# Six gathering stages of a graph network: each gather also waits for the gather two places ahead of it

## The reference

```python
h = relu(layernorm(x)); x = x + attention(h)       # layer 0: softmax over all edges, sums by src
h = relu(layernorm(x)); x = x + edge_mlp(h)        # layer 1: relu(concat(h[src], edge_attr) @ W1a + b1a) @ W1b, means by dst
h = relu(layernorm(x)); x = x + gatv2_twice(h)     # layer 2: logits of h[src] + h[dst] + e, softmax by dst, weighted sums
def edge_conv(x, W1, b1, W2, b2):                  # layer 3: three of these
    m = concat([x[dst], x[src] - x[dst]], axis=-1)
    return segment_max(relu(m @ W1 + b1) @ W2 + b2, dst)
```

## Time and profile before

| | us |
|---|---|
| median of 3 runs | 11882.29 (11880.79 to 11889.4) |
| span of the profiled execution | 11983.4 |
| busy in it: PE | 7468.0 (62%) |
| DVE | 6860.6 (57%) |
| POOL | 6587.1 (55%) |
| ACT | 2573.8 (21%) |

### The profile page before, as it was taken

One profiled execution on the slowest core, in us unless ns is written; L12 is line 12 of the kernel. 1 busy time (PEld: TensorE's weight loads), 2 busy tenths in 40 slices (PEclk: granted clock), 3 DMA queues, 4 the chain that ended last, 5 costly groups with the idle time before them and its releaser, 6 DMA issues. The chain is left out here.

```text
span 11983.4 us, 181872 instructions
## 1 busy us (share of the span) xinstructions
PE 7468.0 (62%) x39289; PEld 6257.1 (52%) x39290; DVE 6860.6 (57%) x13795; ACT 2573.8 (21%) x9089; POOL 6587.1 (55%) x6703
## 2 busy tenths in 40 slices
PE   5944444366665777736565554667777676766676
PEld 4944444355555555524454444655555555555555
DVE  6845444433335888866644445665555555565555
ACT  3500000111111000036600001333333233323332
POOL 0088888466651666613256663326666566646665
PEclk8956666555557888879976666779999899989998
DMA  4355555322223666645444443423333333333333
GB/s 124 73 96 96 96 95 95 98 66 66 67 58 76 216 215 213 219 85 160 128 119 127 127 128 100 113 79 130 129 131 130 118 131 129 129 117 130 131 131 120
DMA packets 829515, 1435.73 MB, mean 120 GB/s; under 512 B 184832, under 2 KB 495468, under 8 KB 788960
## 3 DMA queue, kind: packets, MB, share of 16 engines
q1 hardware_dynamic: 532336, 981.36, 25.8%
q0 software_dynamic: 297072, 453.23, 17.4%
HBM read 1114.85 MB, written 320.07 MB: 120 GB/s over the span
## 5 line engine op out<-in xcount | busy, mean ns | idle before, releaser
L1674 POOL DMA_INDIRECT T<-gather_d,srci x2508 | 2386.0, 951 | 1655.8 <-remote 618.6
L1723 PE MATMUL PS<-T,W 128*128 128x512 f32 x1248 | 816.5, 741 | 1102.5 <-issue 601.4
L882 POOL DMA_INDIRECT added_d<-T,slots x832 | 1293.7, 1555 | 284.0 <-issue 215.6
L1249 PE MATMUL PS<-T,ident 128*128 128x256 f32 (+1 forms) x3328 | 1086.0, 410 | 544.6 <-issue 377.1
L964 DVE TENSOR_TENSOR T<-T,PS 128x128 f32 (+1 forms) x2098 | 561.0, 286 | 1267.7 <-remote 935.2
L1247 PE MATMUL PS<-T 128*128 x3328 | 1050.4, 400 | 347.5 <-issue 343.7
L1198 POOL DMA_INDIRECT T<-wide_d,srci x832 | 844.2, 1015 | 686.0 <-PEq L71 267.6
L987 POOL DMA_INDIRECT T<-gather_d,srci x832 | 822.2, 988 | 583.9 <-issue 232.9
L1249 PEld LDWEIGHTS PS<-T,ident 128*128 128x128 f32 x3328 | 717.7, 244 | 768.7 <-issue 463.9
L1198 POOL DMA_INDIRECT T<-gather_d,srci x832 | 800.4, 962 | 578.8 <-issue 234.5
L1469 PE MATMUL PS<-T 128*128 128x260 f32 (+1 forms) x3328 | 758.5, 384 | 445.8 <-DVEq L1522 392.7
(11 more groups left out here) (254 smaller groups left out, 15227.1 us busy)
## 6 DMA issues: line engine op xcount, KB each, us to landing
T<-quads_d SPq DMA_DIRECT2D x315, 1024.0 KB
T<-edge_rows_d SPq DMA_DIRECT2D x210, 512.0 KB
edge_rows_d<-T SPq DMA_DIRECT2D x209, 512.0 KB
T<-onehot_t_d SPq DMA_DIRECT2D x416, 256.0 KB
T<-gather_d,srci POOLq DMA_INDIRECT x4172
T<-edge_rows_d SPq DMA_DIRECT2D x210, 256.0 KB
onehot_t_d<-T SPq DMA_DIRECT2D x208, 256.0 KB
edge_rows_d<-T SPq DMA_DIRECT2D x208, 256.0 KB
```

Source lines behind the costliest of these rows:

```text
L882: gp.indirect_dma_start(added_d[u][:, :], bass.IndirectOffsetOnAxis(ap=slots[:, k:k + 1], axis=0), part(OUT[r], u), None, compute_op=ALU.a ...
L1249: last = T_.matmul(spot(r, u), ident[:, :], part(R[r], u, width), start=False, stop=True)
L1674: gp.indirect_dma_start(part(R[n % RING], u), None, gather_d[:, :], bass.IndirectOffsetOnAxis(ap=srci[:, k:k + 1], axis=0)).then_inc(rows_ ...
L1723: T_.matmul(bank(2 + i), w2, RT[i], start=True, stop=True).then_inc(products_made.h, 1)
```

## The change

Before each gather of the six stages POOL also waits for the landing of the gather two places ahead of it in the order of the stage. The helper takes group n and place u and finds that gather's semaphore and count. Since a gather can so have two waits, the group's wait for its ring buffer gets an increment of `pool_gate` behind it, to stand on.

```diff
+        def landed_before(gp, n, u):
+
+            m, v = (n, u - 2) if u >= 2 else (n - 1, u + 2)
+            if m >= 0:
+                gp.wait_ge(rows_in[m % RING][v].h, rows_in[m % RING][v].at(16 * (m // RING) + 16))
+
         def edge_mlp_sums():
...
                     for n in range(GROUPS):
                         gp.wait_ge(rows_added.h, rows_added.done(n - RING))
+                        gp.sem_inc(pool_gate.h, 1)
                         for u in range(GROUP):
                             k = LEAD + n * GROUP + u
+                            landed_before(gp, n, u)
                             gp.indirect_dma_start(part(R[n % RING], u), None, gather_d[:, :],
...
+            pool_gate.passed(GROUPS)
...
                         gp.wait_ge(rows_free_again.h, rows_free_again.done(n - RING))
+                        gp.sem_inc(pool_gate.h, 1)
                         for u in range(GROUP):
                             k = step_of(n) + u
+                            landed_before(gp, n, u)
                             gp.indirect_dma_start(part(R[n % RING], u, width), None, table[:, :],
...
-            pool_gate.passed(GROUPS)
+            pool_gate.passed(2 * GROUPS)
...
                     for n in range(GROUPS + 1):
                         gp.wait_ge(edges_made.h, edges_made.done(n - RING))
+                        gp.sem_inc(pool_gate.h, 1)
                         for u in range(GROUP):
                             k = LEAD + n * GROUP + u
+                            landed_before(gp, n, u)
                             gp.indirect_dma_start(part(R[n % RING], u), None, gather_d[:, :],
...
+            pool_gate.passed(GROUPS + 1)
```

## The result

| | before | changed |
|---|---|---|
| median of 4 runs, us | 11881.54 (11862.51 to 11889.4) | 12834.28 (12826.13 to 12848.17) |
| span of the profiled execution, us | 11983.4 | 12835.6 |

The ratio is 1.0803, with a 95% interval of 1.079 to 1.0816. The sign was forecast; the time lies 709 us above the predicted 12125 and 74 us above the range.

What follows compares the result with a forecast made beforehand. Taken as bound by POOL's back-to-back gathers holding up the other engines until the ring fills. Terms -106, +144, -24 and +229 sum to +243 us, span 11983.4 to 12226, forecast 12125 us, range 11700 to 12760 us.

Steps and rivals of the forecast that it cites:

- The sign: Whole kernel: the change makes it slower, chance 0.74, against 0.18 for faster and 0.08 for within 0.2%.
- The wait binds, at 2.75 us for two gathers: POOL, unloaded gathering stage: waiting for landings makes two gathers take 2.75 us instead of 2.49.
- The rival in which it never binds: Six gathering stages: POOL sees landings within 2.49 us of the start, so all stays at 11882 us; chance 0.04.
- The increments cost nothing: POOL's queue, one pool_gate increment per group: taken as 0, with 375 us if every group stopped there.
- Most of the held-up time goes: Gathering stages: the slower gather stream mostly lets the other engines through; edge MLP stage at 1.41 us a gather, -106 us.
- Wide logits, 3.4 us a pair: Wide logits stage, 128 KB gathers beside stores and loads: 3.4 us for two, 1406 against 1262 us, +144.
- Narrow logits, 3.0 us a pair: Narrow logits stage: two gathers take 3.0 us, 1248 against 1272 us, -24.
- Maxima, 12.85 us for eight gathers: Three maxima stages: eight gathers at 1.375 us plus 1.85 us for meeting the 1 MB load; +76 each, +229 together.
- the rival in which gathers pass beside it: Maxima stages: gathers are little delayed by the 1 MB load and keep their pace; sum +14, 11896 us, chance 0.10.
- The carried 0.85%: Whole kernel: the profiled span's 0.85% excess over the median was carried over, turning 12226 us into 12125.
- others held up: Six stages: other engines stay held up, POOL's runs only get longer; sum +869 us, 12750 us, chance 0.24.

Runs made afterwards that it cites:

- e7: Changed kernel with each gather waiting for the landing of the one right ahead, so one gather at a time; 19631.12 us.
- e10: Changed kernel, unedited, run again beside new runs of the kernel before; 12741.65 us, ratio 1.1786 to the kernel before.
- e1: Changed kernel without its landing waits, keeping one pool_gate increment per group; 10825.91 us, ratio 1.0005 to the kernel before.
- e6: Changed kernel with a pool_gate increment ahead of each gather in place of the landing wait; 10826.8 us, ratio 1.0008 to the kernel before.
- e14: Changed kernel with 1 MB and one-hot loads cut to 8 of 128 partitions and each gather's rows stored separately; 11845.19 us (1 run).
- e3: Changed kernel with the 1 MB maxima loads and the one-hot logits loads cut to 8 of 128 partitions; 12067.47 us (1 run).
- e9: Kernel before the change, unedited, profiled again beside the experiments; 10803.36 us (1 run).
- e2: Changed kernel with the landing wait looking three places back, not two; 11428.38 us, ratio 1.0561 to the kernel before.

## Why the sign was right and the size wrong

The step that failed is the price of a landing wait where other transfers run: 3.4 us for two gathers in the wide logits stage, where 3.94 were measured, and 12.85 us for eight gathers in the maxima stages, where 13.7 were measured. The mechanism was right: POOL waits for landings, and that sets the pace.

- *The wait binds, at 2.75 us for two gathers.* Right: 2.77 in the timeline; 2.79 from start to awaiting start in e7; 2.82 over the edge MLP stage of e10. The rival in which it never binds fell.
- *The increments cost nothing.* Right, as far as these runs can tell (e1, e6).
- *Most of the held-up time goes.* As forecast for the maxima stages, only in part for the edge MLP stage: its pace was forecast at 1.41 us a gather, and e10 has 1175 / 832 = 1.41; but 74 us of pauses stayed in the first comparison. -30 in place of -106 us. In the maxima stages, too, some of these waits stayed ("remote" above), without a price that can be seen. This credit exists only against the first comparison's kernel before; beside e10, where the kernel before has no pauses, the same change costs 1930 us and not 953. Since that kernel can run without them, it is not shown that it was the change that took the pauses away.
- *Wide logits, 3.4 us a pair: the worst mis-sized term of a single stage.* 3.94 us were measured (1637 / 416), +382 in place of +144 us. Of the two latencies in the earlier trace rows I took the 3.12 and set the 4.93 aside as a crowd behind a pause that would not last. The 3.12 is close to the median landing in e10, but a group has two late gathers, at 4.33 and 3.89 us, and the wait passes them on. The crowd lasts: the landing that releases POOL also releases SP's store, once a group. With the store split and the load light it would have been 3.33 (e14), about what I took. The landings of L1209 in the wide stage of e10:

```profile
DMA to landing us min/median/max: 2.6/3.2/4.8
```

- *Narrow logits, 3.0 us a pair.* 3.12 (1297 / 416); +29 in place of -24 us, the same mistake in small (the second and third gather of a group landed in 3.16 and 2.99 us in e10, the others in 2.51).
- *Maxima, 12.85 us for eight gathers.* 13.7 us (1432 / 104.5). The meeting with the 1 MB load, taken as 1.85 us, measured 1.93 (e3), and the rival in which gathers pass beside it fell. The Trainium skill (DMA: Bandwidth & Descriptors, on queues, rings and completion order) says that an engine takes turns between queues packet by packet; what I had drawn from it, that a gather is delayed little, did not come true, for a gather that met the load was 2.6 us late. How the engines took turns no trace here shows. The rest was mis-sized: without most of the load eight gathers take 1230 / 104.5 = 11.8 us and not 11.0. 0.16 of it is the step of 2.79. For the rest, the trace of e3 has the awaited landing for 677 gathers of the first maxima stage: 520 of these waited for it, and the other 157 only for the end of the gather before; all but seven start within 0.31 us of whichever came last. So these steps too are landings, of which some come late (2.5 us in the median, a tenth above 2.9, 4.3 at most), and POOL's own pace behind them. How the 0.6 us divide between the two was not taken apart. In all +516 in place of +229 us. The landings of L1688 in that stage:

```profile
DMA to landing us min/median/max: 2.4/2.5/4.3
```

- *The carried 0.85%.* The changed kernel's profiled execution has next to none of it (12835.6 against a median of 12834.28), which is 100 us of the miss. The profiled execution of before was itself a longer one: its rest of the program took 4389.4 us, where e9 took 4346.5 and the changed kernel 4344.6.

By own spans the forecast was +243 and +852 came: 76 (edge MLP), 238 (wide), 53 (narrow) and 287 us (the three maxima stages together) too little, less 45 us that the rest of the program lost. With the 100 us this is the miss of 709. The rival with the nearest number, others held up (12750 us), is not what happened: outside the edge MLP stage, where 74 us of pauses stayed, POOL waits for landings, and the others follow at once.

## What to carry to other kernels

A wait for a transfer's landing costs the latency at its own place in the loop and not the median one (in the wide stage 3.2 us in the median, 4.33 for the second gather of a group), and a transfer that the same landing releases will be beside it each time: look for the queue that wakes on the same event. With a ring of four groups as the only bound, the 1 MB loads cost 14 to 24 us a stage; with two gathers in flight, 201 us. And before a loss in the kernel before is counted as something to win back, see whether it is there in another measurement, on another chip.

## What the runs showed of the hardware that was not expected

- The same kernel took 11881.54 us in one comparison and 10811.54 to 10825.76 us in four others on three chips. Of the 1182 us between the two profiled spans 1139 lie in the six gathering stages; in the timelines it is seen as a lag of 2.95 us (against 0.12) before other engines act on PE's signal, and in the waits as "remote", which stands in both traces of the first comparison and in none of the experiments. Even the changed kernel, which came out alike, has it in the first and not in e10. Neither the rate of gathers nor the loads bring it about by themselves, since e9 has both. What does is open.
- In the wide stage splitting the store saved 42 us and lightening the load 38 us, and the two together saved 253 us.
- TensorE's granted clock in the narrow stage is 0.64 on average in the kernel before (e9) and 0.50 (1.2 GHz) in the changed kernel (e10), where PE waits for landings; its busy time there grew from 803 to 990 us for the same matmuls. With three places ahead (e2) the clock is 0.64 and PE busy 807 us.
